# Attention row maxima in wider units, with a mask product for each head

## The chip, the cores and the metric

One core of one Trainium2 chip runs the whole program in one launch. The metric is the device time of an execution in microseconds (us). The engines are TensorE (PE, with its weight loads as PEld), VectorE (DVE), ScalarE (ACT), GpSimd (POOL) and SyncE (SP), which here issues most DMAs.

## The reference

One transformer layer on x of 2 batches x 1024 tokens x 128 channels, with a layer norm behind each half.

- Attention: q, k, v = x W + b for 16 heads of depth 8; scores = q k^T * scale; a mask that leaves out later keys in chunks of 64 (within a chunk's square a triangle); softmax over the keys; values; output projection; x + attention; layer norm (x1).
- Feed-forward: a router (sigmoid, the best 4 of 8 groups, the best 6 of 32 experts, weights normalised and times 2.5), 32 experts of width 64 and a shared one of width 128, each silu(x1 G) * (x1 U) times a down matrix, summed with the router's weights; x1 + sum; layer norm.

## The kernel before

**Start.** The q and k projections (L1217) leave PSUM through ACT and are split on DVE (the last two of eight on POOL) into three bf16 parts each, stored in a DRAM scratch tensor, and read back as 48 rows for each half of the array: the products of q and k parts, six for each of the 8 depths. `load_q` (L587) and `load_k` (L596) do the reading: for each half a load of 24, of 16 and of 8 rows of 4 KB, 12 loads for a group of four heads. SP issues them, but for the k rows of group 0, which ACT issues. The V projections (L1224) run meanwhile.

**Attention.** Eight groups (2 batches x 4) of four heads. Heads 0 and 1 of a group lie on array rows 0 to 47, heads 2 and 3 on rows 64 to 111. Three streams go through PE.

- Maxima: for each block of 128 queries the scores over its keys, queries on the partitions (L1255), in units of at most one PSUM bank (512 columns); DVE takes the maximum along the keys (L983). `max_units` (L45) makes the units. Part 0 is the 128 keys on the diagonal for two heads at once (2 x 128 columns), which first get the mask by one product of an identity on all 128 rows (L1251); parts 1 and 2 are the keys to the right, up to 512 of them. A group has 48 units: 16 masked, 16 of one head by 512, 8 of one head by 384, 4 of two heads by 256, 4 of two heads by 128. Three banks take turns (`RING`). After a group's last unit DVE joins the parts (L993); PE turns the 32 columns (L1239), ACT copies them, POOL splits them in three (`split_top`), and six DMAs put them into three further rows of q (`store_max`). The last group is done in two halves.
- Exponentials: the scores again, keys on the partitions, now with the maximum among the rows (L1321), and exp on ACT (L880).
- Values: probabilities times V (L1338, fp32, four heads on four column strips of 32), added up in bank 4 (`VALUES`), copied out by ACT.

**Tail.** Four chunks of 512 tokens. A chunk's steps (`CHUNK_STEPS`, L109) are: outputs by token and divided by the sums (4 "out"), turned, projected, residual, statistics, norm, x1 by channel, router logits, 8 routing steps on DVE, and router weights by expert ("comb"). Chunk 0's 20 steps stand between the maxima from unit 6 of group 6 on (`TAIL_FROM`, L135), one after every second unit; the first 11 of chunk 1 follow the last maximum. The experts' loop (68 units, L1353 to L1380) comes after that, and the rest of the tail lies in it.

**Order.** `attention_order` (L160) is a planner: with estimated costs it walks through the three streams and writes down one static order for PE, one for ACT and one for POOL. A unit of maxima goes first whenever it is ready; then exponentials, then values. DVE works in the order of `MSEQ`, made by `max_steps` (L116): units, tops and tail steps one after the other. Every engine runs its list in order.

Of the kernel before, what the change touches and what calls it, by code (L numbers as in the profile page):

```python
# [8 lines left out]
P = 128  # L9
B, T, C = 2, 1024, 128  # L10
HEADS, D = 16, 8
# [5 lines left out]
BANK = 512  # L17
# [7 lines left out]
NG = B * GPB  # L25
# [10 lines left out]
ROWS = 48  # L36
K_EXP = ROWS + 3
ROW_HALF = P // 2
PAIRS = HG // 2
# [5 lines left out]
def max_units(qts):  # L45


    units = []
    for qt in qts:
        k0, n = P * qt, T - P * qt  # L50
        for part, most in ((0, P), (1, BANK), (2, BANK)):
            m = min(n, most)
            if m:
                units += [(js, qt, k0, m, part) for js in ([(0, 1), (2, 3)] if 2 * m <= BANK else [(0,), (2,), (1,), (3,)])]
            k0, n = k0 + m, n - m
    return units
# [30 lines left out]
NE = len(EXPU)  # L87
# [5 lines left out]
NM = len(MAXU[0])  # L93
# [10 lines left out]
def top_of(g, qh):  # L104
    return TOPS.index((g, qh if g >= SPLIT_FROM else None))


QUAD = 4
CHUNK_STEPS = ([("out", t) for t in range(QUAD)] + [("turn", 0), ("proj", 0), ("stat", 0), ("aggr", 0), ("norm", 0),  # L109
                                                   ("x1T", 0), ("logit", 0)]  # L110
               + [("route", t) for t in range(8)] + [("comb", 0)])
# [20 lines left out]


TOP_AFTER = 3
TAIL_FROM = (NG - 2, 6)  # L135
TOPS_BEFORE = [[t for t in TOPS if t[0] < g_] for g_ in range(NG)]
MSEQ = max_steps()
MAX_AT = {step: r for r, step in enumerate(step for step in MSEQ if step[0] in ON_BANK)}
# [21 lines left out]
def attention_order():  # L160


    ev, vv = ([(g, n) for g in range(NG) for n in range(k)] for k in (NE, NB))
    hop, rows_latency, load = 240, 6000, 6000
    exp_slack, mask_slack = 300, 600
    t = 0.0
    clock = {"act": 0.0, "pool": 5000.0}
    dve = 0.0
# [11 lines left out]
    i = {"e": 0, "m": 0, "v": 0}  # L180
    streams = {"e": ev, "m": MSEQ, "v": vv}
    far = 1e18
# [55 lines left out]
    def ready_m():  # L238
        k = i["m"]
        kind, g, n = MSEQ[k]  # L240
        out = 0
        if kind in ON_BANK and MAX_AT[kind, g, n] >= RING:
            out = read.get(RSEQ[MAX_AT[kind, g, n] - RING], far)
        if kind == "unit":
            if g >= NS and n == 0:
                out = max(out, e_done.get((g - NS, NE - 1), far) + load)
        elif kind == "top":
            group, qh = TOPS[g]
            out = max(out, m_done[group, NLOW - 1 if qh == 0 else NM - 1] + 350)
        elif kind == "out":  # L250
            out = max(out, copied.get((GPB * (g // 2 + 1) - 1, g % 2), far))
        elif kind == "turn":
            out = max(out, dve_done["out", g])
        elif kind == "proj":
            out = max(out, act_done.get(("turn", g), far))
        elif kind == "norm":
            out = max(out, root_done.get(g, far))
        elif kind == "x1T":
            out = max(out, dve_done["norm", g])
        elif kind == "logit":  # L260
            out = max(out, read.get(("x1T", g, 0), far))
        elif kind == "comb":
            out = max(out, dve_done["route", g])
        return out
# [12 lines left out]
    while any(i[k] < len(s) for k, s in streams.items()):  # L277
        run_sides(t)
        ready = [(f(), rank, k) for rank, (k, f, s) in enumerate(
            (("m", ready_m, MSEQ), ("e", ready_e, ev), ("v", ready_v, vv))) if i[k] < len(s)]  # L280
        now = [c for c in ready if c[0] <= t]
        side = next_side()
        if not now and side and min(ready)[0] > side[0]:
            run_sides(side[0])
            continue
        when, _, k = min(now, key=lambda c: c[1]) if now else min(ready)
        t = max(t, when)
        if k == "e":
            g, n = ev[i[k]]
            b, pairs, m = EXPU[n]  # L290
            t += len(pairs) * max(m / 2.4 + 25, 110)
            e_done[g, n] = t
            todo["act"].append(("x", g, n, t + hop, 2 * len(pairs) * m / 1.2 + 170))
        elif k == "m":
            kind, g, n = step = MSEQ[i[k]]
            if kind == "unit":
                js, _, _, m, part = MAXU[g][n]
                t += len(js) * max(m / 2.4 + 10, 105) + 120 * (part == 0)
                dve = max(dve, t + hop) + len(js) * m / 0.96 + 125
                read[step] = m_done[g, n] = dve  # L300
                if n in (NLOW - 1, NM - 1):
                    dve += 300
            elif kind == "top":
                t += 150
                todo["act"].append(("top", g, 0, t + hop, 300))
            else:
                t += {"out": 330, "turn": 330, "proj": 1000, "x1T": 330, "logit": 900, "comb": 330}.get(kind, 0)
                if kind in ("turn", "logit", "comb", "x1T"):
                    todo["act"].append((kind, g, n, t + hop, 620))
                ready_at = t + hop + (1000 if kind == "x1T" else 0)  # L310
                if kind in on_dve:
                    dve = max(dve, ready_at) + on_dve[kind]
                    dve_done[kind, g] = dve + 100
                    read[step] = dve + 100
                else:
                    read[step] = ready_at + 900
                if kind == "aggr":
                    todo["pool"].append(("root", g, 0, dve + hop, 1100))
        else:
            g, b = vv[i[k]]  # L320
            t += width(b) * 4 / 2.4 + 70
            v_done[g, b] = t
            qh = BLOCKS[b][0]
            if b == HALF_END[qh]:
                todo["act"].append(("c", g, qh, t + hop, 620))
        if k != "m" or MSEQ[i[k]][0] in ON_BANK:
            pe_order.append((k, *streams[k][i[k]]) if k != "m" else (k, 0, i[k]))
        i[k] += 1
# [8 lines left out]
def build(nc, a, out):  # L337
# [3 lines left out]
    with ctx:  # L341
# [8 lines left out]
        identb, mask_qk = sb("identb", [P, P], bf16), sb("mask_qk", [P, P], bf16)  # L350
# [15 lines left out]
        rows_k = sb("rows_k", [P, NS, PAIRS * T], bf16)  # L366
# [18 lines left out]
        with ExitStack() as early:  # L385

            def first(name, shape, dt):
# [13 lines left out]
                           for s in range(2) for v in (rows_q, rows_k))  # L401
# [4 lines left out]
                                                                                    n=BANK)  # L406


        at = [0]
# [16 lines left out]
        def bank(n, cols=BANK, at=0):  # L426
            return ps[:, n * BANK + at:n * BANK + at + cols]
# [22 lines left out]
        v_ready = sem("v_ready")  # L450
# [136 lines left out]
        def load_q(eng, g):  # L587
            b, r = g // GPB, slice((g % GPB) * STRIP, (g % GPB + 1) * STRIP)
            s = g % NS
            part = scr[0, b, :, r, :].rearrange("h (d f p) t -> f h d (p t)", d=D, f=2)  # L590
            for f in range(2):
                for at, n, src in ((0, 24, part[f]), (24, 16, part[f, 0:2]), (40, 8, part[f, 0])):
                    eng.dma_start(rows_q[ROW_HALF * f + at:ROW_HALF * f + at + n, s, :],
                                  src).then_inc(rows_loaded[s], 16)

        def load_k(eng, g):  # L596
            b, r = g // GPB, slice((g % GPB) * STRIP, (g % GPB + 1) * STRIP)
            s = g % NS
            part = scr[1, b, :, r, :].rearrange("h (d f p) t -> f h d (p t)", d=D, f=2)
            for f in range(2):  # L600
                for at, n, src in ((0, 24, part[f, 0:1].to_broadcast([3, D, PAIRS * T])),
                                   (24, 16, part[f, 1:2].to_broadcast([2, D, PAIRS * T])), (40, 8, part[f, 2])):
                    eng.dma_start(rows_k[ROW_HALF * f + at:ROW_HALF * f + at + n, s, :],  # L603
                                  src).then_inc(rows_loaded[s], 16)

# [603 lines left out]
        def _(pe):  # L1209
# [10 lines left out]
            for n in range(NC):  # L1220
# [3 lines left out]
                    mm = pe.matmul(bank(VPROJ[n], P, t * P), xT[:, tt * P:(tt + 1) * P], wv[:, :], start=True, stop=True)  # L1224
                mm.then_inc(v_projected, 1)

            def max_step(kind, g, n):

                r = MAX_AT[kind, g, n]
# [12 lines left out]
                if kind != "unit":  # L1242
                    tail_step(kind, g, n)
                    return
                if r == 0:
                    pe.wait_ge(masks_loaded, 32)
                js, qt, k0, m, part = MAXU[g][n]
                s, dst = g % NS, step_bank((kind, g, n), len(js) * m)
                if part == 0:

                    pe.matmul(dst.rearrange("p (j m) -> p j m", m=m), identb[:, :],  # L1251
                              mask_qk[:, :].unsqueeze(1).to_broadcast([P, len(js), P]), start=True, stop=False)
                for at, j in enumerate(js):
                    f, p = ROW_HALF * (j // PAIRS), j % PAIRS * T
                    mm = pe.matmul(dst[:, at * m:(at + 1) * m], rows_q[f:f + ROWS, s, p + qt * P:p + (qt + 1) * P],  # L1255
                                   rows_k[f:f + ROWS, s, p + k0:p + k0 + m], start=part > 0,
                                   stop=part > 0 or at == len(js) - 1)
                mm.then_inc(max_scores, 1)

            def tail_step(kind, n, i):  # L1260
# [210 lines left out]
```

## Time and profile before

| | us |
|---|---|
| Median of 3 runs | 496.4 (492.8 to 497.02) |
| The profiled execution | 494.91 |
| Its span | 493.1 |
| First unit of maxima | 34.1 |
| Join of group 0, join of the last half group | 60.0, 272.9 |
| Experts' loop from its third unit on | 319.1 |
| PE busy | 444.3 (90%) |
| DVE busy | 350.3 (71%) |
| ACT busy | 223.1 (45%) |
| POOL busy | 141.9 (29%) |
| Mean granted clock | 0.901 |

The span runs from the first instruction to the last; 1.8 us of the execution lie outside of it. The granted clock is TensorE's share of its full speed in a stretch: 1.0 is 2.4 GHz, 0.5 is 1.2 GHz. A matmul's record ends when its results have landed, so that records overlap; what a product costs the stream is read from one start to the next.

### The profile page before, as it was taken

The page shows a single profiled execution, that of the slowest core. Times are in us where ns is not written, and L with a number is a line of the kernel's source. Part 1 is how long each engine was busy: PE and PEld are TensorE (multiplying, and loading weights), DVE is VectorE, ACT ScalarE, POOL GpSimd, SP SyncE. Part 2 cuts the span into 40 slices and gives each one's busy share as a digit, 9 for nine tenths or more (in the row PEclk, how much of TensorE's full clock was granted, in tenths as well). Part 3 has the DMA queues.
Part 4 walks back from the last instruction along what each step waited for, and adds up shares of the span by engine and source line. Part 5 has one row for each costly group of instructions (what it writes and reads, how often), then busy time and mean ns, then how long its engine had stood idle before and what let it go on. Part 6 is the DMA issues. An engine that isn't in the chain of part 4 may idle for free.

```text
span 493.1 us, 7763 instructions
## 1 busy us (share of the span) xinstructions
PE 444.3 (90%) x2665; PEld 210.1 (43%) x2665; DVE 350.3 (71%) x848; ACT 223.1 (45%) x300; POOL 141.9 (29%) x244
## 2 busy tenths in 40 slices
PE   5429999999999999999799879899999999999992
PEld 2302232323333232433223323367676676666660
DVE  2619988888988888777987331286768869965863
ACT  4520016766857767677215369723242243223220
POOL 4061333756746362533213442400000000000000
PEclk9955558999999999998858869999999999999997
DMA  3434214420010101000000030033323322543330
GB/s 117 163 137 148 89 42 141 128 72 26 27 52 24 45 20 50 3 1 1 7 2 2 1 87 1 1 97 103 107 72 100 111 90 86 148 133 105 109 106 21
DMA packets 27031, 34.22 MB, mean 69 GB/s; under 512 B 5745, under 2 KB 16113, under 8 KB 26993
## 3 DMA queue, kind: packets, MB, share of 16 engines
q1 hardware_dynamic: 25862, 33.00, 21.7%
q10 hardware_dynamic: 1130, 0.74, 0.5%
q8 instruction: 21, 0.34, 0.3%
q14 instruction: 18, 0.14, 0.1%
HBM read 29.07 MB, written 4.46 MB: 68 GB/s over the span
## 4 chain that ended last, share of the span: by engine, by line
PE 73%; DVE 13%; DMA 4%; issue 3%; ACTq 3%; ACT 2%; POOL 2%; DVEq 0%; SPq 0%; POOLq 0%
PE ps L1338 13%; PE ps L1255 13%; PE ps L1380 11%; DVE mx L983 9%; PE ps L1353 6%; PE ps L1355 6%; PE ps L1354 6%; PE ps L1321 6%; PE ps L1251 6%; DMA rows_k<-scratch 2%; ACT probs L880 2%; ACTq L568 2%; PE ps L1268 1%; DMA wq<-in_wqT 1%; ACTq L603 1%
## 5 line engine op out<-in xcount | busy, mean ns | idle before, releaser
L983 DVE TENSOR_REDUCE mx<-ps 128x2 f32<-128x256 f32 (+3 forms) x384 | 191.0, 552 | 43.8 <-PE ps L1255 42.4
L880 ACT ACTIVATE probs<-ps 128x1024 f32<-128x1024 f32 (+2 forms) x160 | 142.8, 939 | 76.8 <-PE ps L1321 69.9
L1255 PE MATMUL ps<-rows_k,rows_q 48*128 48x128 bf16 (+3 forms) x576 | 117.6, 313 | 5.2 <-DVE mx L983 3.2
L1338 PE MATMUL ps<-probs,Vg 128*32 128x512 f32 (+3 forms) x768 | 86.8, 526 | 1.2 <-POOL probs L754 1.0
L923 ACT ACTIVATE rows_q<-ps 128x512 f32<-128x512 f32 x68 | 40.7, 599 | 97.3 <-PE ps L1355 94.7
L1255 PEld LDWEIGHTS ps<-rows_k,rows_q 48*128 48x128 bf16 x576 | 35.5, 97 | 91.6 <-DVE mx L983 65.9
L750 POOL TENSOR_SCALAR_AFFINE_SELECT probs<-probs 64x512 f32<-64x512 f32 x64 | 42.4, 662 | 110.4 <-ACT probs L880 108.9
L1353 PE MATMUL ps<-x1hi,w_hi 128*128 128x512 f32 x136 | 74.0, 544 | 0.0
L1321 PE MATMUL ps<-rows_q,rows_k 51*128 51x512 bf16 (+3 forms) x384 | 67.8, 347 | 4.0 <-ACT probs L880 3.9
L1380 PE MATMUL ps<-rows_k,w_down 128*128 128x512 f32 x136 | 69.5, 593 | 0.7 <-DVE rows_k L1199 0.7
L1194 DVE TENSOR_TENSOR rows_q<-ps,rows_q 128x512 f32<-128x512 f32 x64 | 44.1, 689 | 36.2 <-PE ps L1380 34.9
L1251 PE MATMUL ps<-mask_qk,identb 128*128 128x256 bf16 x128 | 40.3, 315 | 18.2 <-DMA rows_k<-scratch 15.7
L798 POOL TENSOR_TENSOR rstd<-ve,half 128x4 f32<-128x4 f32 x8 | 8.1, 1015 | 167.8 <-DVE ve L1043 167.8
L1355 PE MATMUL ps<-x1hi,w_lo 128*128 128x512 f32 x136 | 53.6, 394 | 0.0
L1354 PE MATMUL ps<-x1lo,w_hi 128*128 128x512 f32 x136 | 53.5, 393 | 0.0
L1199 DVE TENSOR_TENSOR rows_k<-comb_rows,rows_q 128x512 f32<-128x512 f32 x64 | 44.3, 692 | 2.2
L1251 PEld LDWEIGHTS ps<-mask_qk,identb 128*128 128x128 bf16 x128 | 12.5, 98 | 54.6 <-DVE mx L983 23.2
L1321 PEld LDWEIGHTS ps<-rows_q,rows_k 51*128 51x128 bf16 x384 | 22.8, 96 | 23.2 <-ACT probs L880 15.1
L1353 PEld LDWEIGHTS ps<-x1hi,w_hi 128*128 128x128 f32 x136 | 25.6, 188 | 15.6 <-issue 11.6
L1354 PEld LDWEIGHTS ps<-x1lo,w_hi 128*128 128x128 f32 x136 | 25.6, 189 | 14.3 <-issue 11.3
L1380 PEld LDWEIGHTS ps<-rows_k,w_down 128*128 128x128 f32 x136 | 25.5, 190 | 7.6 <-DVE rows_k L1199 1.8
L1355 PEld LDWEIGHTS ps<-x1hi,w_lo 128*128 128x128 f32 x136 | 25.6, 188 | 5.8
(105 smaller groups left out, 326.6 us busy)
## 6 DMA issues: line engine op xcount, KB each, us to landing
comb_rows<-weights SPq DMA_DIRECT2D x128, 128.0 KB, 3.0
scratch<-oT SPq DMA_DIRECT2D x8, 384.0 KB, 5.6
w_raw<-in_unitT SPq DMA_DIRECT2D x17, 128.0 KB, 5.7
rows_q<-scratch SPq DMA_DIRECT2D x16, 96.0 KB
rows_k<-scratch SPq DMA_DIRECT2D x14, 96.0 KB
w_down<-in_unitT SPq DMA_DIRECT2D x1, 1088.0 KB, 6.3
xT<-in_xT SPq DMA_DIRECT2D x4, 256.0 KB, 5.6
rows_q<-scratch SPq DMA_DIRECT2D x16, 64.0 KB
```

What stands on the lines that cost most here:

```text
L880: act.activation(dst, src, ACT.Exp).then_inc(exps_ready, 1)
L983: dve.tensor_reduce(to, src, AX.X, ALU.max).then_inc(max_read, 1)
L1194: dve.tensor_tensor(au[:, i % 2, :], bank(2 + i % 2), sg[:, i % 2, :], ALU.mult).then_inc(gated_ready, 1)
L1199: dve.tensor_tensor(hh[:, i % 2, :], comb_rows[:, p % CB, :], au[:, i % 2, :], ALU.mult).then_inc(hidden_ready, 1)
L1251: pe.matmul(dst.rearrange("p (j m) -> p j m", m=m), identb[:, :], mask_qk[:, :].unsqueeze(1).to_broadcast([P, len(js), P]), start=True, st ...
L1255: mm = pe.matmul(dst[:, at * m:(at + 1) * m], rows_q[f:f + ROWS, s, p + qt * P:p + (qt + 1) * P], rows_k[f:f + ROWS, s, p + k0:p + k0 + m] ...
L1321: mm = pe.matmul(bank((NE * g + n) % 2 * 2 + f, m, a_ * m), rows_k[r, s, p * T + kt * P:p * T + (kt + 1) * P], rows_q[r, s, p * T + qh * B ...
L1338: mm = pe.matmul(ps[STRIP * j:STRIP * (j + 1), VALUES * BANK:VALUES * BANK + m], Vg[:, g % 2, kt, j, :], probs[:, (NB * g + b) % SLOTS, j, ...
L1353: pe.matmul(dst, w_hi[:, u, w], x1hi[:, cols], start=True, stop=False)
L1354: pe.matmul(dst, w_hi[:, u, w], x1lo[:, cols], start=False, stop=False)
L1355: pe.matmul(dst, w_lo[:, u, w], x1hi[:, cols], start=False, stop=True).then_inc(ready, 1)
L1380: pe.matmul(bank(ACC), w_down[:, u, :], hh[:, i % 2, :], start=u == 0, stop=u == NU - 1).then_inc(down_done, 1)
```

## The change

- Units: part 0 is now up to 256 keys for two heads, a full bank. Each head gets its row product first (start) and then its own mask product of 128 columns, added onto the diagonal. A group then has 40 units: 16 masked (14 of 2 x 256, 2 of 2 x 128), 12 of one head by 512, 4 by 384, 4 of two heads by 256, 4 of two heads by 128.
- Row loads: the source's dimensions are in the order depth, part instead of part, depth, for q and k alike; sizes and bytes stay.
- 22 products of 128 rows x 128 columns on 512 columns (`keep_clock`), whose result nobody reads, after the V projections; and one more ahead of each unit among the first 56 entries of the ring (40 in group 0, 15 in group 1; the 56th is a top).
- All steps of the tail stand behind the last maxima: chunk 0's 20, then chunk 1's 11.
- The planner holds a unit back that is more than 1.6 groups ahead of the exponentials, and prices a mask at 105 ns for each head.

```diff
-        for part, most in ((0, P), (1, BANK), (2, BANK)):
+        for part, most in ((0, BANK // PAIRS), (1, BANK), (2, BANK)):
...
+WARM, WARM_UNITS = 22, 56
...
-TAIL_FROM = (NG - 2, 6)
+TAIL_FROM = (NG, 0)
...
+    lead = 1.6
...
+        if kind == "unit" and g + n / NM - i["e"] / NE > lead and i["e"] < len(ev):
+            return far
...
-                t += len(js) * max(m / 2.4 + 10, 105) + 120 * (part == 0)
+                t += len(js) * (max(m / 2.4 + 10, 105) + 105 * (part == 0))
...
-            part = scr[0, b, :, r, :].rearrange("h (d f p) t -> f h d (p t)", d=D, f=2)
+            part = scr[0, b, :, r, :].rearrange("h (d f p) t -> f d h (p t)", d=D, f=2)
+
             for f in range(2):
-                for at, n, src in ((0, 24, part[f]), (24, 16, part[f, 0:2]), (40, 8, part[f, 0])):
+                for at, n, src in ((0, 24, part[f]), (24, 16, part[f, :, 0:2]), (40, 8, part[f, :, 0])):
...
-            part = scr[1, b, :, r, :].rearrange("h (d f p) t -> f h d (p t)", d=D, f=2)
+            part = scr[1, b, :, r, :].rearrange("h (d f p) t -> f d h (p t)", d=D, f=2)
             for f in range(2):
-                for at, n, src in ((0, 24, part[f, 0:1].to_broadcast([3, D, PAIRS * T])),
-                                   (24, 16, part[f, 1:2].to_broadcast([2, D, PAIRS * T])), (40, 8, part[f, 2])):
+                for at, n, src in ((0, 24, part[f, :, 0:1].to_broadcast([D, 3, PAIRS * T])),
+                                   (24, 16, part[f, :, 1:2].to_broadcast([D, 2, PAIRS * T])), (40, 8, part[f, :, 2])):
...
+            def keep_clock(n):
+                for _ in range(n):
+                    pe.matmul(bank(VALUES), identb[:, :], parts[:, 0, 0, :], start=True, stop=True)
+
+            pe.wait_ge(masks_loaded, 32)
+            pe.wait_ge(v_ready, 1)
+            keep_clock(WARM)
...
-                if r == 0:
-                    pe.wait_ge(masks_loaded, 32)
+                if r < WARM_UNITS:
+                    keep_clock(1)
...
-                if part == 0:
-
-                    pe.matmul(dst.rearrange("p (j m) -> p j m", m=m), identb[:, :],
-                              mask_qk[:, :].unsqueeze(1).to_broadcast([P, len(js), P]), start=True, stop=False)
                 for at, j in enumerate(js):
                     f, p = ROW_HALF * (j // PAIRS), j % PAIRS * T
                     mm = pe.matmul(dst[:, at * m:(at + 1) * m], rows_q[f:f + ROWS, s, p + qt * P:p + (qt + 1) * P],
-                                   rows_k[f:f + ROWS, s, p + k0:p + k0 + m], start=part > 0,
-                                   stop=part > 0 or at == len(js) - 1)
+                                   rows_k[f:f + ROWS, s, p + k0:p + k0 + m], start=True, stop=part > 0)
+                    if part == 0:
+                        mm = pe.matmul(dst[:, at * m:at * m + P], identb[:, :], mask_qk[:, :], start=False, stop=True)
```

## Rows read from the trace of the kernel before

**Rows 1.** The page's span, and the granted clock (tenths) in 40 slices.
```profile
span 493.1 us, 7763 instructions
...
PEclk9955558999999999998858869999999999999997
```

**Rows 2.** Stretches: length; PE, PEld, DVE, ACT, POOL busy; clock; DMA share; GB/s.
```profile
88.20:199.40 111.20, 108.86 (x944) 36.98 (x943) 96.28 (x196) 76.80 (x94) 62.78 (x112) 1.00 0.15 48
115.70:143.10 27.40, 26.95 (x237) 9.19 (x233) 23.91 (x49) 18.98 (x24) 17.76 (x29) 1.00 0.11 34
199.40:272.90 73.50, 68.47 (x495) 23.90 (x493) 59.70 (x165) 36.77 (x48) 25.95 (x48) 0.84 0.01 3
272.90:319.10 46.20, 38.43 (x290) 15.03 (x290) 10.12 (x30) 32.22 (x41) 18.48 (x34) 0.85 0.10 24
```

**Rows 3.** Stretches of the start, columns as in Rows 2.
```profile
18.00:23.00 5.00, 0.42 (x4) 0.23 (x3) 2.41 (x4) 0.70 (x2) 0.00 (x0) 1.00 0.40 113
24.00:30.00 6.00, 0.00 (x0) 0.00 (x0) 0.00 (x0) 3.52 (x6) 3.32 (x3) 0.50 0.26 93
34.00:60.00 26.00, 24.66 (x92) 7.04 (x92) 23.45 (x49) 0.00 (x0) 5.64 (x11) 0.50 0.38 128
60.00:72.00 12.00, 11.93 (x53) 3.91 (x54) 10.73 (x25) 0.26 (x1) 5.74 (x11) 0.50 0.13 36
78.00:86.00 8.00, 7.49 (x58) 2.07 (x58) 7.41 (x14) 5.39 (x6) 2.95 (x6) 1.00 0.63 174
```

**Rows 4.** Timeline of DVE: joins of groups 0 and 1 and of the last half group.
```profile
59.99 0.26 DVE L993 TENSOR_REDUCE mxj<-mx 128x32 f32<-128x96 f32 x1
...
88.17 0.26 DVE L993 TENSOR_REDUCE mxj<-mx 128x32 f32<-128x96 f32 x1
...
272.85 0.21 DVE L993 TENSOR_REDUCE mxj<-mx 128x16 f32<-128x48 f32 x1
```

**Rows 5.** Timelines of the DMA queues: one load of 8 rows; ACT's six loads.
```profile
19.20 0.42 SPq L593 DMA_DIRECT2D rows_q<-scratch  x1
...
19.38 4.51 ACTq L603 DMA_DIRECT2D rows_k<-scratch  x6
```

**Rows 6.** The page's DMA issues: KB each, median us from issue to landing.
```profile
comb_rows<-weights SPq DMA_DIRECT2D x128, 128.0 KB, 3.0
```

**Rows 7.** Timeline of PE at clock 0.5: V projections, first mask, row pair, next mask.
```profile
14.69 3.73 PE L1224 MATMUL ps<-wv,xT 128*128 128x128 f32 x32
34.11 0.39 PE L1251 MATMUL ps<-mask_qk,identb 128*128 128x256 bf16 x1 [15.69 <-DMA rows_k<-scratch]
34.44 0.39 PE L1255 MATMUL ps<-rows_k,rows_q 48*128 48x128 bf16 x2
34.76 0.40 PE L1251 MATMUL ps<-mask_qk,identb 128*128 128x256 bf16 x1
```

**Rows 8.** Timeline of PE at clock 1.0: row pairs of 128 and 256 columns, masks.
```profile
144.07 0.28 PE L1255 MATMUL ps<-rows_k,rows_q 48*128 48x128 bf16 x2
144.28 0.28 PE L1251 MATMUL ps<-mask_qk,identb 128*128 128x256 bf16 x1
144.50 0.28 PE L1255 MATMUL ps<-rows_k,rows_q 48*128 48x128 bf16 x2
...
147.60 0.39 PE L1255 MATMUL ps<-rows_k,rows_q 48*128 48x256 bf16 x2
147.92 0.28 PE L1251 MATMUL ps<-mask_qk,identb 128*128 128x256 bf16 x1
```

**Rows 9.** Waits from 115.7 to 143.1: total us, times, longest.
```profile
PEld ps L1255 <- DVE mx L983: 8.7, 14, 0.8
```

**Rows 10.** Timelines of DVE and ACT: chunk 0's first and last step, chunk 1's last.
```profile
204.35 0.25 DVE L1014 RECIPROCAL rec<-ps 128x16 f32<-128x16 f32 x1
...
243.26 0.57 ACT L914 COPY combT<-ps 32x512 f32<-32x512 f32 x1 [3.93 <-PE ps L1302]
...
298.81 0.28 ACT L909 ACTIVATE work<-ps 128x128 f32<-128x128 f32 x1 [0.29 <-PE ps L1297]
```

## The prediction

> **What bounds the kernel now.** I read the clock line first [rows 1]: TensorE's granted clock is 0.9 to 1.0 but for two stretches, the first maxima (slices 3 to 6) and the end of attention (slices 20 to 24). Then the stretches [rows 2]. In the steady part a group takes 27.4 us: PE is busy for 26.95 of them, DVE for 23.91, ACT for 18.98. So PE sets the pace there, though not alone: its weight loads waited 8.7 us, in 14 waits, for DVE to free a bank [rows 9]. The last two groups of maxima take 73.5 us instead of 55, with the clock at 0.84: chunk 0's tail stands between their units on DVE. Behind the last join [rows 4] come 46.2 us until the experts' loop, in which ACT is busiest (32.22). The start stands last [rows 3, 7]: the V projections end at 18.4, and PE then idles until 34.11, for the k rows of group 0. The clock was 1.0 until 23, was 0.5 from 24 on, and stayed there through 34 to 72, although PE was busy nearly always, with products on 48 rows and a few on 128; it stood at 1.0 from 78 on, after the fp32 value products had joined in.
>
> **The change part by part.** All sums are against the profiled execution: span 493.1, 1.8 outside it, 494.9 in all, which is 1.5 below the median of 496.4.
>
> *Row loads.* ACT issues its six loads in 4.51 us from 19.38, and the rows are there at 34.11, 10.2 us after the last issue [rows 5, 7]. The DMA share between 24 and 30 is 0.26 while two queues load [rows 3]: some four of 16 engines work. The 8-row load, whose outermost dimension is the depth already, is issued in 0.42 us; six like it from 19.38 end at 22. A load that spreads lands 3.0 us after its issue [rows 6]. That gives 25.1 instead of 34.1: -9.0 us; the bounds are 0 and -10.2 (the whole wait behind the last issue). The Trainium skill (DMA: Bandwidth & Descriptors, section "Why a DMA increments its semaphore by 16 and not by 1") has the number of engines as the largest up to 16 that divides the outermost sizes of both sides: three for 24 rows and two for 16 before, eight for each now. By it and the page's 27 GiB/s an engine the 24 rows take an estimated 0.4 us, landing would be bound by issue alone, and the sum would be -9.6. The trace agrees with few engines (the 0.26). The loads of later groups are shorter as well and on no path: they are issued a group ahead. SP is free sooner for the expert weights that POOL splits ahead of the first top; this costs nothing and can only help.
>
> *The 22 products.* From the row pairs [rows 8]: two of 128 columns and the change to the next mask take 0.21 us, two of 256 take 0.32, so 256 columns cost 0.107 and the change between a product on 48 rows and one on 128 another 0.107. A product on 512 columns is 0.21 us, and 22 are 4.7: 18.4 to 23.1, inside the wait. The two waits ahead of them (masks, V's first copy) stand where PE idles anyhow. Cost 0; were the clock 0.5 they would end at 28 and hold all of PE's list back by 3.
>
> *Units and masks.* Old masked unit: 0.22 for the mask and the change, 0.21 for the pair: 0.43, and 16 make 6.9 us. New one: two times (0.107 + 0.107 for a row product, 0.053 + 0.107 for its mask), 0.75; 14 of these and two of 0.64 make 11.8. Gone are four units of 512 columns (0.32) and four of 384 (0.27): 2.4. A group costs PE up to 2.5 us more, or 3.7 if half of what is gone ran beside products on the other array half. The lower bound is 0, since the columns are the same and PE waits for DVE for up to 8.7 us in a group [rows 9], while DVE has eight instructions less. Between 0 and 3.7 two rows pull apart (PE busy at 98%, weight loads waiting for DVE); I take 1.5, so 28.9 us for a steady group.
>
> *Group 0* now has a 512-column product ahead of each unit. At clock 1.0 a masked unit is 0.75 + 0.21 = 0.96, the two small ones 0.85, one of 512 columns 0.21 + 0.107 + 0.32 = 0.64, of 384 0.59, two by 256 0.64, two by 128 0.53: 13.5 + 1.7 + 7.7 + 2.4 + 2.6 + 2.1 = 30.0 us on PE, with little beside it. Before, 34.1 to 60.0 is 25.9 [rows 4, 7]: +4.1. The lower bound is DVE's 23.45 of busy time: -2.5.
>
> *Group 1*: 15 units at some 0.8 us, 12.0, and 25/40 of 28.9, 18.1: 30.1 against 28.2 [rows 4]: +1.9.
>
> *Groups 2 to 5*: 4 x 28.9 = 115.6 against 111.2 [rows 2]: +4.4.
>
> *Groups 6 and 7* lose the tail between their units: 57.8 against 73.5: -15.7. What is queued behind: the tail's 31 steps now come one after the other on DVE behind the last maxima, chunk 1's behind chunk 0's routing.
>
> *The end.* Chunk 0 took 38.9 us from its first step to its last [rows 10] with 40 reductions among them, some 20 us by DVE's 96.28 for 4 x 48 of them [rows 2]: between 18.8 and 38.9, I take 29. Chunk 1 took 26.0 from the last join to its logits [rows 4, 10]; between that and the same share of it, 13, I take 20. With 2 for the last top that is 51 us against 46.2: +4.8, bounds 34 and 67. The exponentials that are left (1.6 groups at 18.98 of ACT, 30 us) fit beside it. The loop then starts behind a nearly idle PE at a lower clock: I put +1.5 (0 to 3).
>
> *The lead* only fixes what the priorities gave before (exponentials began at 72, when the maxima were at 1.4 groups): 0, for planning only.
>
> Sum: -9.0 + 4.1 + 1.9 + 4.4 - 15.7 + 4.8 + 1.5 = -8.0. Span 485, execution 487 us, 1.9% below the median.
>
> **The rivals.**
>
> *The changes of shape hide* (0 instead of 1.5 a group): seven groups give 10.5 back, 476 us. For it: DVE frees the banks in 14 of the waits. Against it: PE's 98%. [...]
>
> *The clock is lost at the start: slower.* PE idles again between 23.1 and 25.1. If the granted clock is at 0.5 when group 0 begins, nothing in the rows promises that it rises before the values: it stayed at 0.5 from 34 to 72 with mask products in the stream [rows 3]. At 0.5 a mask of 256 columns and its change take 0.33 and a pair of 128 0.32 [rows 7], so 128 columns are 0.107 and a change 0.11. A masked unit with its extra product is 2 x (0.32 + 0.22) + 0.43 = 1.51, one of 512 columns 1.08, and group 0 is 48 us instead of 30; group 1's 15 units add 7. That is +25: 512 us. For it: the same idling took the clock before, after 5 us. Against it: 2 us of idling is less than that, and the extra products are on all 128 rows. It decides at the first unit.
>
> *The tail chain is long*: 67 us instead of 51, or all changes of shape exposed (3.7 instead of 1.5): both come to +15 or +16, 502 us. For it: 31 steps hop between four engines, and static PE order puts exponentials between them. Against it: nothing else is left on DVE.
>
> *The loads do not spread*: rows at 34 as before, 496 at best.
>
> **How the numbers follow.** About 1% is what a measurement of this kernel can tell from no change: faster is below 491, slower above 501. The forecast, 487, has 0.44; its own range, 476 to 499, comes from 0.5 to 2.5 for the shapes (-7 to +7) and -5 to +6 at the end; 0.30 of it is faster, 0.12 the same, 0.02 slower. Shapes hidden: 0.14, faster. Clock lost: 0.21, slower. Long tail or shapes exposed: 0.16, slower 0.11, same 0.05. Loads as before: 0.05, same 0.03, slower 0.02. Together faster 0.44, same 0.20, slower 0.36. The range, 474 to 513, takes in the cases on both sides.
>
> **What would show it.** Loads: the first unit near 25 instead of 34.1. Clock: 1.0 over 25 to 70; 0.5 there with group 0's join past 70 means the second rival. Shapes: joins of groups 2 to 7 28.9 us apart; 27.4 is the first rival, 31 the third. Tail: the last join near 259 and the loop some 51 us behind it, with ACT idle before the loop. I am wrong if the joins keep their distance and yet the loop begins no sooner, or if the loop's own 174 us change.

## The result and the profile after

| | Before | After |
|---|---|---|
| Executions beside each other, us | 492.8 to 497.02 (median 496.6) | 529.09, 529.75, 543.44, 554.09 (median 536.6) |
| Profiled execution, its span | 494.91, 493.1 | 529.75, 527.8 |

The ratio is 1.068 with an interval of 1.059 to 1.077: slower, outside the range of the forecast (474 to 513). Ratios leave out executions whose clock was low for longer than in a kernel's fastest ones; where the mask stands with each head this spread is part of the finding, so all times are given.

From the page of the changed kernel: span, busy time of the engines, clock in 40 slices.

```profile
span 527.8 us, 7977 instructions
...
PE 491.9 (93%) x2801; PEld 230.5 (44%) x2806; DVE 351.7 (67%) x784; ACT 224.1 (42%) x300; POOL 141.7 (27%) x244
...
PEclk9955555589999999998999798999999999999997
```

PE is busy for 47.6 us more than before (444.3), DVE for 1.4. The clock is at its lower level, 1.2 GHz, for two more slices at the start than in [rows 1], that is until 109 us instead of 78, and lower in a few later ones. The stretches say what was done in them (columns as in [rows 2]):

```profile
18.70:23.60 4.90, 4.85 (x23) 2.06 (x21) 1.81 (x3) 0.17 (x1) 0.00 (x0) 1.00 0.42 127
23.60:27.80 4.20, 0.01 (x1) 0.00 (x0) 0.00 (x0) 3.58 (x6) 1.16 (x1) 0.96 0.47 160
27.80:77.20 49.40, 48.18 (x136) 12.54 (x139) 25.58 (x41) 0.00 (x0) 14.98 (x20) 0.50 0.27 84
77.20:109.40 32.20, 31.51 (x115) 8.95 (x120) 18.37 (x31) 5.27 (x7) 4.60 (x9) 0.50 0.33 98
109.40:116.30 6.90, 6.47 (x52) 2.35 (x44) 6.25 (x12) 4.30 (x6) 1.80 (x3) 1.00 0.07 21
...
146.10:175.80 29.70, 29.14 (x242) 11.05 (x234) 23.74 (x41) 17.21 (x22) 16.14 (x27) 1.00 0.12 33
...
236.30:301.20 64.90, 63.61 (x471) 22.58 (x474) 47.48 (x84) 37.93 (x47) 24.52 (x47) 0.89 0.01 2
```

The first line is the 22 products at clock 1.0, the second PE's wait for the k rows, the third group 0 at 0.5: 49.4 us, of which DVE (23.45 of 26.00 us busy before, [rows 3]) is busy for 25.58. The steady group (146.1 to 175.8) takes 29.7 at full clock, the last two 64.9 with the clock at 0.89. Joins on DVE's timeline, for [rows 4] (group 0, 1, 2, 5, and the last half group):

```profile
77.19 0.26 DVE L998 TENSOR_REDUCE mxj<-mx 128x32 f32<-128x96 f32 x1
116.27 0.26 DVE L998 TENSOR_REDUCE mxj<-mx 128x32 f32<-128x96 f32 x1
146.09 0.27 DVE L998 TENSOR_REDUCE mxj<-mx 128x32 f32<-128x96 f32 x1
...
236.32 0.27 DVE L998 TENSOR_REDUCE mxj<-mx 128x32 f32<-128x96 f32 x1
...
301.17 0.21 DVE L998 TENSOR_REDUCE mxj<-mx 128x16 f32<-128x48 f32 x1
```

The start on PE's timeline, for [rows 7]: the wait, and then the first unit with starts 0.22 apart, where the clock is already 0.5.

```profile
18.70 4.91 PE L1236 MATMUL ps<-oT,identb 128*128 128x512 bf16 x21
27.83 0.61 PE L1236 MATMUL ps<-oT,identb 128*128 128x512 bf16 x1 [4.22 <-DMA rows_k<-scratch]
28.37 0.29 PE L1266 MATMUL ps<-rows_k,rows_q 48*128 48x128 bf16 x1
28.59 0.29 PE L1269 MATMUL ps<-mask_qk,identb 128*128 128x128 bf16 x1
```

The third unit of the experts' loop on PE's timeline:

```profile
353.84 0.50 PE L1365 MATMUL ps<-x1hi,w_hi 128*128 128x512 f32 x1
```

The mean granted clock of this execution, 0.901, is that of the kernel before: its time at the lower level grew with its span, and the rest of what was added is work at the upper one. Where the 34.7 us of span went, step by step (span 527.8 against 493.1; the loop is counted from its third unit):

| Step | Forecast | Measured | From |
|---|---|---|---|
| Row loads, first unit | -9.0 | -6.3 | 27.8 for 34.1 |
| Group 0 | +4.1 | +23.5 | 49.4 for 25.9 |
| Group 1 | +1.9 | +10.9 | 39.1 for 28.2 |
| Groups 2 to 5 | +4.4 | +8.8 | 120.05 for 111.24 |
| Groups 6 and 7 | -15.7 | -8.6 | 64.85 for 73.44 |
| Last join to the loop | +4.8 | +6.4 | 52.7 for 46.2 |
| The loop | +1.5 | 0.0 | 174.0 for 174.0 |

### The profile page after: what moved, and what is told of

Read it like the earlier page. It is cut to its first block, busy times and chain, and to the rows that moved or that the text cites. A ratio compares the mean times of both kernels' runs of the same rounds, so it can differ in the third digit from the quotient of the medians.

```text
span 527.8 us, 7977 instructions
## 1 busy us (share of the span) xinstructions
PE 491.9 (93%) x2801; PEld 230.5 (44%) x2806; DVE 351.7 (67%) x784; ACT 224.1 (42%) x300; POOL 141.7 (27%) x244
## 4 chain that ended last, share of the span: by engine, by line
PE 84%; DVE 7%; DMA 2%; issue 2%; ACT 2%; ACTq 1%; POOL 1%; DVEq 0%; SPq 0%; POOLq 0%
PE ps L1266 18%; PE ps L1350 13%; PE ps L1392 11%; PE ps L1269 9%; PE ps L1365 6%; PE ps L1333 6%; PE ps L1367 6%; PE ps L1366 6%; PE ps L1236 5%; DVE mx L988 2%; PE ps L1280 1%; DVE x L1053 1%; ACT probs L885 1%; DMA wq<-in_wqT 1%; DMA rows_k<-scratch 1%
## 5 line engine op out<-in xcount | busy, mean ns | idle before, releaser
L988 DVE TENSOR_REDUCE mx<-ps 128x2 f32<-128x512 f32 (+3 forms) x320 | 190.5, 634 | 88.1 <-PE ps L1269 63.9
L885 ACT ACTIVATE probs<-ps 128x1024 f32<-128x1024 f32 (+2 forms) x160 | 144.7, 941 | 101.7 <-PE ps L1333 97.1
L1266 PE MATMUL ps<-rows_k,rows_q 48*128 48x256 bf16 (+3 forms) x512 | 137.5, 324 | 4.8 <-DVE mx L988 2.4
L1266 PEld LDWEIGHTS ps<-rows_k,rows_q 48*128 48x128 bf16 x512 | 42.1, 97 | 97.9 <-DVE mx L988 46.6
L1333 PE MATMUL ps<-rows_q,rows_k 51*128 51x512 bf16 (+3 forms) x384 | 65.0, 345 | 6.8 <-ACT probs L885 6.4
L1199 DVE TENSOR_TENSOR rows_q<-ps,rows_q 128x512 f32<-128x512 f32 x64 | 44.1, 689 | 35.5 <-PE ps L1392 34.9
L1269 PE MATMUL ps<-mask_qk,identb 128*128 128x128 bf16 x256 | 62.7, 245 | 0.0
L1269 PEld LDWEIGHTS ps<-mask_qk,identb 128*128 128x128 bf16 x256 | 25.1, 98 | 40.6 <-issue 21.3
L1236 PE MATMUL ps<-oT,identb 128*128 128x512 bf16 x72 | 36.5, 550 | 4.3 <-DMA rows_k<-scratch 4.2
L1333 PEld LDWEIGHTS ps<-rows_q,rows_k 51*128 51x128 bf16 x384 | 19.1, 96 | 32.5 <-issue 17.7
```

Of the source, the lines that this page charges most:

```text
L885: act.activation(dst, src, ACT.Exp).then_inc(exps_ready, 1)
L988: dve.tensor_reduce(to, src, AX.X, ALU.max).then_inc(max_read, 1)
L1236: pe.matmul(bank(VALUES), identb[:, :], parts[:, 0, 0, :], start=True, stop=True)
L1269: mm = pe.matmul(dst[:, at * m:at * m + P], identb[:, :], mask_qk[:, :], start=False, stop=True)
L1333: mm = pe.matmul(bank((NE * g + n) % 2 * 2 + f, m, a_ * m), rows_k[r, s, p * T + kt * P:p * T + (kt + 1) * P], rows_q[r, s, p * T + qh * B ...
```

## The experiments

**The products made longer, and left out.** The first theory was the second rival of the forecast: the clock is lost while PE waits for the rows.

```diff
-WARM, WARM_UNITS = 22, 56
+WARM, WARM_UNITS = 44, 56
```

and, in the other kernel,

```diff
-WARM, WARM_UNITS = 22, 56
+WARM, WARM_UNITS = 0, 0
```

> The changed kernel with 44 products that nobody reads instead of 22 after the V projections, so that they end near 28.2, where the rows of group 0 have landed (27.8). Theory A: the clock was lost in the 4.2 us in which PE idled between these products and the first unit, and at 0.5 the full-array products ahead of the units are what PE spends its time on. Then the clock is 1.0 at the first unit, group 0 takes 30 us instead of 49.4, group 1 30 instead of 39.1, and the time is 29 us below the changed kernel: about 501. Theory B: the clock is lost by what the units themselves are (products on 48 rows and changes of shape), whatever stood before them. Then it falls to 0.5 a few us behind the first unit, group 0 takes over 45 us, and the time stays at 528 to 531.

> The changed kernel without any of the products that nobody reads, neither the 22 nor those ahead of 55 units. Theory A: the clock is 0.5 from 24 on as in the kernel before, and the units run without 0.43 us each: group 0 49.4 - 40 x 0.43 = 32 us, group 1 39.1 - 15 x 0.43 = 33 us, the time 24 us lower, about 506. Theory C: the extra products are no loss, since the units at half clock with a mask for each head are what PE spends its time on: groups 0 and 1 together stay over 80 us and the time above 520.

With 44 products the four executions took 529.41, 529.14, 510.73 and 550.57 us; without any, 549.87, 517.79, 531.94 and 527.21. Stretches of the kernel with 44, in its execution of 529.41:

```profile
28.30:58.80 30.50, 30.50 (x141) 11.27 (x141) 23.91 (x40) 0.00 (x0) 14.96 (x20) 1.00 0.43 136
58.80:70.00 11.20, 11.20 (x61) 4.52 (x60) 7.84 (x14) 0.25 (x1) 2.38 (x5) 1.00 0.01 2
71.00:84.00 13.00, 12.83 (x52) 3.46 (x55) 9.39 (x16) 5.25 (x6) 2.20 (x4) 0.50 0.51 153
...
92.00:134.00 42.00, 42.00 (x211) 11.70 (x207) 21.70 (x37) 16.72 (x22) 15.96 (x29) 0.50 0.11 33
```

Theory A holds for the start: the clock is 1.0 at the first unit and group 0 takes 30.5 us, where 30 was forecast. Yet the total fell in one execution of four alone: 510.73 at a mean clock of 0.954, the others at 0.900, 0.900 and 0.861. At 71 the clock fell, about one us behind the last of the products ahead of units, as the starts on PE's timeline tell (PE idles for 0.30 us there):

```profile
69.89 0.38 PE L1236 MATMUL ps<-oT,identb 128*128 128x512 bf16 x1
70.20 0.34 PE L1266 MATMUL ps<-rows_k,rows_q 48*128 48x384 bf16 x2
70.84 1.32 PE L1266 MATMUL ps<-rows_k,rows_q 48*128 48x384 bf16 x3 [0.30 <-DVE mx L988]
72.09 0.29 PE L1269 MATMUL ps<-mask_qk,identb 128*128 128x128 bf16 x1
```

The mask at 72.09 takes 0.29, which is the duration at 0.5 (0.23 at 1.0). The clock rose for some us at 84, and was 0.5 again from 92 to 134, where PE's records cover 42.00 of 42.00 us. Group 2 gave back most of what groups 0 and 1 had gained, and the later ones the rest: its join came at 137.3 against 146.1 after 91.1 against 116.3, and the last join at 299.2 against 301.2. Without the products, in the slowest of the four executions, groups 0 and 1 took 30.2 and 32.6 us (32 and 33 expected by A; C had over 80 for both), and the clock was at 0.5 from 92 to 133, 140 to 177 and 242 to 283. So A and C both fail on the total: something in the stream itself does not hold the clock.

**Loads alone, tail alone, both.** (The edits are the load hunks of the change and `TAIL_FROM = (NG, 0)`, on the kernel before.)

> The kernel before with one part of the change, the row loads with the depth outermost. Theory: first unit at 27.8 as in the changed kernel instead of 34.1, the rest of the start moved by as much (group 0's join near 53.7), the time 6 us lower: about 490. Rival: what is gained at the first unit is lost by group 1 (its rows or its banks late), the joins of groups 2 and later stand where they stood, and the time is 496.

> The kernel before with one part of the change, chunk 0's tail behind the last maxima. Theory: groups 6 and 7 take 55 to 58 us instead of 73.5, the end from the last join to the loop 48 to 51 instead of 46.2, the time 11 to 16 lower: 480 to 485. Rival: the tail's DVE work and its hops only change place, the loop begins where it began (near 319), and the time is 494 to 498.

> The kernel before with two parts of the change: the row loads with the depth outermost and chunk 0's tail behind the last maxima. If the two gains are independent (6.6 and 7.3 us alone), the time is 14 us below before, 480 to 482. If the earlier start only moves work into the end, it is 486 to 488.

Loads: 488.3 us, ratio 0.987 (0.983 to 0.990). Tail: 487.9, ratio 0.985 (0.981 to 0.989). Both: 482.3, ratio 0.972 (0.968 to 0.977); the gains add up. The first unit came at 28.15 with the loads alone; DMA issues of ACT and PE's first unit there, for [rows 5] and [rows 7]:

```profile
19.51 4.50 ACTq L603 DMA_DIRECT2D rows_k<-scratch  x6
```

```profile
28.15 0.39 PE L1251 MATMUL ps<-mask_qk,identb 128*128 128x256 bf16 x1 [9.54 <-DMA rows_k<-scratch]
```

The issue did not get shorter (4.50 for 4.51); the rows land 4.1 us behind the last issue instead of 10.2. The tail alone brought groups 6 and 7 to 57.2 us (join of the last half at 256.9, of group 5 at 199.65), as forecast, but its end to the third unit of the loop took 56.0 instead of 46.2 and the loop 2.4 more; of the 16.2 us gained there, 3.8 are left in this execution, the longest of four (491.11 for 494.91).

**The units alone, and the masks alone.** If it is the stream, which part of it?

```diff
-                    pe.matmul(dst.rearrange("p (j m) -> p j m", m=m), identb[:, :],
-                              mask_qk[:, :].unsqueeze(1).to_broadcast([P, len(js), P]), start=True, stop=False)
...
+                    if part == 0:
+                        mm = pe.matmul(dst[:, at * m:at * m + P], identb[:, :], mask_qk[:, :], start=False, stop=True)
```

This is the edit of the masks alone (units of 128 keys stay); the units alone have the wide part 0 of the change as well. Both also take over the planner's price of 105 ns for each mask. Every kernel here with a mask behind each head's row has this price, and every other has the old one, so the two go together throughout.

> The kernel before with the new units alone: two heads by 256 keys, a mask product for each head, and the planner's price for it; loads, tail and start as before, and no product that nobody reads. Theory D: a stream of the new units does not get the clock back to 1.0 as the old ones did. Then it stays at 0.5 beyond 100 us (78 before), again in later groups, the joins of groups 1 and 2 come over 10 us late each, executions differ by 10 us and more, and the time is 515 to 540. Theory E: the new units cost their changes of shape alone, and the clock was lost by the products that nobody reads. Then the clock is 1.0 from about 80 on and stays there, group 0 takes 30, group 1 31, the later groups 2.4 each more than before, and the time is 505 to 514 with executions within 2 us.

> The kernel before with a mask product for each head of a unit (128 columns, behind the head's row product) in place of one for both, units of 128 keys as before: 16 x 0.21 us more of PE in a group by the products' starts. If the masks for each head are what keeps the clock down, it stays at 0.5 beyond 100 and the time is over 520. If the width of the units does it, the clock is 1.0 from about 80 on as before, and the time is 500 to 515, for 1 to 2.4 us of changes of shape in each group.

Units with their masks: 528.01 to 558.06 us, ratio 1.073 (1.063 to 1.083). Masks alone: 528.93 to 539.76, ratio 1.074 (1.065 to 1.083), the clock at 0.5 until 116 and again from 126 to 136. In the profile of the units alone it rose at 91, not beyond 100 as theory D had it, but was 0.5 again from 190 to 220 and between 0.50 and 0.83 from 230 to 290. Theory E's 514 is passed by all executions. The mask for each head, with its price, loses as much at the old width as the wide units with it do.

**Two masks ahead of both rows.** The masks alone add 16 products to a group, and two changes between products on 48 and on 128 rows to each masked unit. This variant keeps the products and takes these changes away (and leaves the planner's price as it was before):

```diff
                 if part == 0:
-                    pe.matmul(dst.rearrange("p (j m) -> p j m", m=m), identb[:, :],
-                              mask_qk[:, :].unsqueeze(1).to_broadcast([P, len(js), P]), start=True, stop=False)
+                    for at in range(len(js)):
+                        pe.matmul(dst[:, at * m:at * m + P], identb[:, :], mask_qk[:, :], start=at == 0, stop=False)
```

> The kernel before with two mask products of 128 columns, one for each head, both ahead of both rows: as many products as with the mask behind each head's row, but two changes between 48 and 128 rows in a unit where that has four. If the changes of shape make the loss, the clock is back at 1.0 near 80, and the time is 494 to 500. If the number of products makes it, the clock is 0.5 beyond 100 and the time is over 515.

496.2 us, ratio 1.000 (0.997 to 1.003). The same 36 us of both kernels, first with the masks behind each head's row, then with both masks ahead:

```profile
80.00:116.00 36.00, 35.83 (x183) 10.51 (x182) 19.76 (x41) 15.05 (x19) 11.81 (x22) 0.50 0.32 90
```

```profile
80.00:116.00 36.00, 34.88 (x314) 11.69 (x312) 32.07 (x65) 24.32 (x30) 19.27 (x34) 1.00 0.40 111
```

PE is busy in both, by 35.8 and 34.9 us; the program is 13.6 us further in the second, by the joins of group 1. With the same products in the other order the clock is twice as high, and 314 of them run instead of 183. So the number of products is not the cause: it is the order. That the changes of shape inside a unit do it is argued, not shown alone, for the planner's price moves units against exponentials and values as well (from the first exponentials on, 436 of the 666 places in PE's list hold another entry), and no run has one without the other. What the changes cost at full clock is shown: both kernels are at 1.00 through groups 3 to 5, which take 91.9 us with the masks behind the rows (joins at 139.73 and 231.64) and 83.8 with both ahead (116.35 and 200.12). That is 2.7 us a group, where 32 changes of 0.107 would make an estimated 3.4.

**The wide units with a shared mask.** On the kernel with loads and tail:

```diff
-        for part, most in ((0, P), (1, BANK), (2, BANK)):
+        for part, most in ((0, BANK // PAIRS), (1, BANK), (2, BANK)):
...
-                    pe.matmul(dst.rearrange("p (j m) -> p j m", m=m), identb[:, :],
+                    pe.matmul(dst.rearrange("p (j m) -> p j m", m=m)[:, :, 0:P], identb[:, :],
...
+                    for c0, c1 in ([(0, P), (P, m)][:m // P] if part == 0 else [(0, m)]):
```

The row products of a masked unit are split at 128 keys. The Trainium skill (Advanced Engine Details and Errata, section "PSUM Accumulation (`has_written` bits)") says that a product without the start mark adds where something has been written since the mark and overwrites elsewhere; so split, each product meets one kind only. No run here shows what an unsplit one does.

> The kernel before with row loads, late tail and the wide units of the change, but one mask product for both heads ahead of the rows, as before (the rows of a masked unit then come as two products of 128 keys for each head). If the mask for each head is what keeps the clock down, this one gets it back near 76 like the kernel with loads and tail alone, a masked unit takes 0.54 us of PE for 256 keys where the old units took 0.59, a group is up to 0.9 us shorter, and the time is 475 to 482. If the wide units do it, the clock is 0.5 beyond 100 and the time is over 500.

476.0 us, ratio 0.957 (0.952 to 0.961): the fastest of all, 4.3% below the kernel before. Two stretches of it, an early one at the lower level and groups 2 to 5:

```profile
54.60:73.00 18.40, 17.37 (x95) 6.92 (x93) 15.29 (x27) 4.24 (x5) 3.30 (x7) 0.50 0.15 45
...
82.90:186.90 104.00, 102.47 (x990) 39.19 (x989) 92.25 (x164) 72.59 (x89) 60.19 (x107) 1.00 0.13 40
```

The same four groups of the changed kernel, also at 1.00:

```profile
116.27:236.32 120.05, 117.85 (x959) 44.02 (x959) 94.31 (x164) 74.72 (x91) 61.45 (x110) 1.00 0.12 34
```

Four groups take 104.0 us, against 111.3 with the old units (loads and tail) and 120.05 in the changed kernel: 26.0, 27.8 and 30.0 each. At full clock the mask for each head thus costs 4.0 us a group beside a shared one on the same wide units. And the width is worth 1.8 us a group (0.9 was expected from the products' starts; DVE's eight instructions less, 92.25 for 96.33, may be the rest, which was not separated).

**The changed kernel with the shared mask**, its products that nobody reads kept (22, then 44 of them after the V projections):

> The changed kernel with one mask product for both heads ahead of the rows in place of one for each head; the wide units, the 22 products, the 55 ahead of units, loads, tail and lead stay. If the products that nobody reads cost on their own, they are at clock 0.5 as in the changed kernel, group 0 takes 41 us (40 x 0.43 on top of 24), group 1 33, the clock is back from the first values on, and the time is 495 to 505. If the masks were the whole loss, the time is that of the same kernel without these products, 475 to 482.

> The same kernel as before (the changed one with a mask product for both heads), with 44 products after the V projections instead of 22, so that they reach the rows' landing. If the 26 us that the products ahead of the units cost there came from running at clock 0.5, they now run at 1.0 and are nearly free: a unit of two heads by 256 takes 0.54 + 0.32 us, group 0 some 28 us beside DVE's 24, as long as without these products at 0.5 (27), group 1 likewise, and the time is 474 to 480. If the products cost their columns whatever the clock, groups 0 and 1 stay over 75 us and the time over 490.

With 22: 502.0 us (nine of ten executions 500.27 to 505.26; the tenth took 543.31 at a mean clock of 0.742, so a shared mask does not rule the loss out), ratio 1.014 (1.011 to 1.018). With 44: 478.4, ratio 0.965 (0.960 to 0.971). Group 0 with 22, and then with 44:

```profile
27.80:72.60 44.80, 43.52 (x146) 12.29 (x148) 25.56 (x40) 0.00 (x0) 14.34 (x20) 0.50 0.30 92
```

```profile
27.40:55.70 28.30, 28.30 (x159) 10.44 (x156) 24.55 (x41) 0.00 (x0) 14.91 (x20) 1.00 0.46 147
```

At 0.5 the products cost 26 us against the kernel without them (502.0 - 476.0; 29 by the ratios; the lead is in this sum too); at 1.0 they keep the clock and gain nothing (28.3 us for group 0 against 26.7 without them at 0.5, where DVE sets the pace). With 44 the clock fell here too, from 68.8 to 75.7, and came back behind the first values (72.24). So the fall at 71 in the first experiment is not the masks' doing; the stretch from 92 to 134 at 0.5 is what this kernel does not have.

**44 products and the old units**, none ahead of units, with loads and tail:

> The same two parts, and 44 products that nobody reads between the V projections and the first unit (to some 28 us), none ahead of the units. If the old units hold a clock that was 1.0 at the first of them, group 0 takes 24 us (what DVE needs) instead of 26, the exponentials begin 2 us sooner, and the time is 477 to 479. If the clock falls to 0.5 inside group 0 with these units too, the time is as without the 44 products, 480 to 482.

485.0 us (481.76 to 487.31), ratio 0.978 (0.972 to 0.984), no better than without them. The clock was 1.0 at the first unit and fell at 34, inside group 0: old units do not hold it either until the values come. They only regain it, and keep it, from then on (72).

## Why the prediction was wrong

**The step that failed is the clock.** The sum put every product of the maxima at 1.0 from the first unit on, because the 22 products were to hold the clock, and had no term for its falling later. The profiled execution had 0.5 from 27.5 to 109.4. Group 0 ran at 0.5 in the kernel before as well, but without a 512-column product ahead of each unit. The span is 42.7 us above the forecast's 485.1: groups 0 and 1 make 28.4 of that (88.5 us for 60.1), groups 6 and 7, at a clock of 0.89, 7.1, groups 2 to 5 4.4, the loads 2.7, and the end and the loop together 0.1. The second rival, which had the clock lost at the start, foresaw 25 of these 28.4. But holding the clock over the start did not mend the kernel: with 44 products three of four executions still took 529 to 551 us, and in the profiled one of these the clock was lost again from 92 on.

**Loads: mechanism right, size off.** The price of an issue was too low: the sum took the 0.42 us of the 8-row load for all, and the six still took 4.53. The landing behind the last issue fell to 3.9 (27.83 less 23.95). -6.3 instead of -9.0. (The -9.6 that the prediction sets beside it is given without its terms.)

**The 22 products** were hidden as forecast (18.7 to 23.6). They did not do what they stand for: the clock went to 0.5 at 27.5, 0.3 us before the first unit. The forecast allowed for 2 us of idling, because it had the rows land at 25.1; it was 4.2.

**Group 0: the working was right, its clock was not.** At 1.0 the same sequence takes 30.5 us (44 products) against 30.0 forecast; at 0.5 it took 49.4, against 48 in the second rival. This rival had 0.21 and its mechanism is the one that came for the start.

**Units and masks: the size was right at full clock, the clock was not.** The sum priced a mask for each head by the changes of shape at full clock alone, 0 to 3.7 us a group, and took it that the clock comes back with the values, as in [rows 3], and stays. A masked unit of the changed kernel, on PE and on its weight loads:

```profile
150.72 0.28 PE L1266 MATMUL ps<-rows_k,rows_q 48*128 48x256 bf16 x1
150.93 0.23 PE L1269 MATMUL ps<-mask_qk,identb 128*128 128x128 bf16 x1
151.10 0.28 PE L1266 MATMUL ps<-rows_k,rows_q 48*128 48x256 bf16 x1
151.31 0.23 PE L1269 MATMUL ps<-mask_qk,identb 128*128 128x128 bf16 x1
151.47 0.29 PE L1266 MATMUL ps<-rows_k,rows_q 48*128 48x128 bf16 x4
```

```profile
150.93 0.10 PEld L1269 LDWEIGHTS ps<-mask_qk,identb 128*128 128x128 bf16 x1
151.09 0.09 PEld L1266 LDWEIGHTS ps<-rows_k,rows_q 48*128 48x128 bf16 x1
151.31 0.10 PEld L1269 LDWEIGHTS ps<-mask_qk,identb 128*128 128x128 bf16 x1
```

From 150.72 to 151.47 are 0.75 us, the price that was forecast. At every change the weight load begins with its product, not ahead of it, and takes the 0.1 us that a change costs. Within a pair of row products it is otherwise: there the second load runs beside the first product, though both heads lie on the same rows. In the kernel before the two loads of the first pair of [rows 8] take 0.11 us together, where one takes 0.10:

```profile
144.06 0.11 PEld L1255 LDWEIGHTS ps<-rows_k,rows_q 48*128 48x128 bf16 x2
```

The Trainium skill (TensorE: Matmul & The Clock Gate, section "The mechanism" of Part 3) says that a weight load overlaps products under way only where its row group differs from theirs. The trace agrees for the changes between 48 and 128 rows, with 0.10 for the load and 0.107 for the change, and not for the pair. At full clock all changes are exposed: 30.0 us a group, 2.2 more than the old units take with loads and tail alone, where 1.5 was forecast; the first rival (changes hide) is refuted by it. These 2.2 are two terms of opposite sign, -1.8 for the width and +4.0 for the masks, an estimated 32 us over eight groups. That is about what the masks cost in the fastest executions with 44 products: 510.73 us with a mask for each head against 476.2 with a shared one, 34.5 apart. What the forecast had no case for lies on top: the other three executions with 44 took 18 to 40 us more than their fastest, at a lower mean clock. Of the five profiled kernels with a mask behind each head's row, four lost the clock for 10 us or more between their first values and the join of group 5 (with 44 products from 92 to 136, masks alone from 126 to 136), and none of the profiled ones without did. The fifth is the changed kernel itself: its clock came back at 109.4, 4.1 us behind its first values (105.31), and stayed until 246. Masks alone cost 34 to 45 us on the kernel before (528.93 to 539.76 against a median of 495.24), and the changed kernel is 27 us or more above the same kernel with a shared mask (529.1 against 502.0).

**Group 1** follows: 39.1 us, with the clock at 0.5 until 109.4. The second rival had 37.1 for it (30.1 and 7).

**Groups 6 and 7 and the end.** The tail's step was right where it stands alone: 57.2 us for a forecast of 57.8. In the changed kernel it is 64.9, at a clock of 0.89. The end took 52.7 where 51 was forecast. The third rival's long chain did not come: 52.7 is far from 67.

**The lead** was costed at nothing and was not tried alone. The units alone (no lead) and the changed kernel without extra products (with it) both begin the exponentials 1.5 groups into the maxima (81.87 between joins at 65.52 and 97.63; 75.11 between 58.75 and 91.32), so it is not what delays them.

By comparisons with the kernel before, then, the change is made of: loads -6.7 us, tail -7.3 alone (-13.7 for both), wide units with a shared mask -7.9 on top (21.6 below), the products at half clock +29 on top of that (1.014 against 0.957), and the masks for each head (with the planner's price) at least +27 more.

**Left open:** why the clock falls where it does in a given execution, and whether the changes of shape or the order that the planner's price makes keep it down. The kernels with a mask for each head lie 11 to 40 us apart from one execution to the next, and what tips one of them was not found.

## What to carry to other kernels

Price an added product by the order that it stands in, not by its columns: group products that use the same rows of the array, because here each change between 48 and 128 rows cost a weight load in the open, 0.1 us, and four of the five profiled kernels with four changes in a unit also lost the clock again. A filler that is to keep the clock must reach the moment at which the real work starts: here the clock fell 0.3 us ahead of it, and what was nearly free at 1.0 cost 26 us; and work that is paced by another engine at half clock, as group 0 by DVE, did not need one. Test a bundle of edits one by one: here the loads and the tail were worth 14 us and the width 8, and the masks and the products hid all of it. Change a planner's price in a run of its own: here it went with the masks, and its share is not known.

## What the runs showed of the hardware

The clock was at 1.2 GHz for 42 us in which PE's records leave no gap (92 to 134 with 44 products, busy 42.00 of 42.00). With masks behind each head's row it was at 1.2 GHz over 36 us with PE busy for 35.83, and with both masks ahead at 2.4 GHz with PE busy for 34.88: the busy share does not tell the two apart. With 44 products it fell at 71, about one us behind the last of the products ahead of units (69.89), with no idling of PE over 0.3 us around it. A change between products on 48 and on 128 rows exposed a weight load of 0.10 us, and two loads for the same rows took 0.11 us together. And the order of a source's dimensions changed when the rows landed (3.9 to 4.1 us behind the last issue instead of 10.2) and not what their issue took (4.50 to 4.53 us).
